# Delaying one step of a feed-forward eviction loop, and moving a quantization pass from VectorE to GpSimd

## The reference, cut

```python
def bitlinear158(x, w, b):
    xq = act_quant(rms_norm(x))      # round(x * 127/max|x|) / scale, per row
    wq = weight_quant(w)             # -1, 0, 1 times mean|w|
    return einsum('bsd,od->bso', xq, wq) + b

xn = layernorm(x)                                   # 4 x 4096 x 2048
h = silu(bitlinear158(xn, w1, b1))                  # 8192 inner columns
h = gelu(h, approximate=False)
h = layer_norm(h, ln_g, ln_b)
ffn = bitlinear158(h, w2, b2)                       # back to 2048
out = x + attention(xn) + ffn
```

## Time and profile before

| | before |
|---|---|
| median of 2 runs | 11771.39 us (11726.16 to 11816.61) |
| profiled execution | 11743.26 us |
| its span on the slowest core, core 4 | 11741.7 us |
| spans of the eight cores | 11662.1 to 11741.7 us |
| mean granted clock, core 4 | 0.765 |
| busy share PE / DVE / ACT / POOL | 45% / 31% / 19% / 2% |

### The profile page before, as it was taken

How to read it: one execution, slowest core, us unless ns; L and a number is a source line. 1 busy time by engine, 2 the same in 40 slices (tenths; PEclk the granted TensorE clock), 3 DMA queues, 4 the chain that set the end, 5 groups by cost and what they waited for, 6 DMA issues and landing times.

```text
span 11741.7 us, 91769 instructions; the slowest of 8 cores (11662.1 to 11741.7 us)
## 1 busy us (share of the span) xinstructions
PE 5257.5 (45%) x28008; PEld 3029.0 (26%) x28008; DVE 3670.1 (31%) x8144; ACT 2251.6 (19%) x4838; POOL 230.3 (2%) x214
## 2 busy tenths in 40 slices
PE   0000023454497434515455463545545465555656
PEld 0000022111133112303334242433334244222222
DVE  5421132111200122272626354362626343112020
ACT  0164442000011112212031211212031220111110
POOL 0000000111000000000000000000000000000000
PEclk9999966767688666757778686767778687777879
DMA  7789925777513554202323242322323234432324
GB/s 258 258 261 188 176 87 88 93 92 93 86 46 57 82 91 84 93 18 108 126 97 140 90 146 77 117 106 108 120 100 143 83 138 152 117 104 82 112 68 140
DMA packets 898720, 1356.88 MB, mean 116 GB/s; under 512 B 561984, under 2 KB 750784, under 8 KB 806080
## 3 DMA queue, kind: packets, MB, share of 16 engines
q1 hardware_dynamic: 495520, 1233.56, 33.3%
q0 software_dynamic: 402720, 117.45, 10.0%
HBM read 1325.70 MB, written 142.61 MB: 125 GB/s over the span
## 4 chain that ended last, share of the span: by engine, by line
DMA 35%; PE 28%; DVE 20%; ACT 7%; issue 6%; DVEq 4%; SPq 1%; ACTq 0%; POOLq 0%
PE PB L1053 9%; DMA fST<-w1q_scr 8%; DMA qW<-w2t 5%; PE PB L628 5%; PE PB L746 4%; DMA kWC<-wk 3%; DMA qW<-w1t 3%; PE PB L1461 2%; DMA tVB<-v_scr 2%; DMA fW<-w2q_scr 2%; PE PB L848 2%; DVE fTF L1354 2%; DMA q3WC<-wq 2%; DMA kt_scr<-kKO 2%; DMA y<-tOB 2%
## 5 line engine op out<-in xcount | busy, mean ns | idle before, releaser
L1053 PE MATMUL PB<-fXQT,fST 128*128 128x256 bf16 x8192 | 1289.9, 326 | 897.8 <-DMA fST<-w1q_scr 897.8
L1053 PEld LDWEIGHTS PB<-fXQT,fST 128*128 128x128 bf16 x8192 | 905.8, 115 | 1265.5 <-issue 1041.6
L848 PE MATMUL PB<-fQ,fW 128*128 128x256 bf16 x8192 | 993.7, 284 | 238.2 <-DMA fW<-w2q_scr 226.6
L848 PEld LDWEIGHTS PB<-fQ,fW 128*128 128x128 bf16 x8192 | 819.8, 102 | 414.7 <-issue 291.9
L628 PE MATMUL PB<-xnT,kWC 128*128 128x512 bf16 x2048 | 584.4, 455 | 646.0 <-ACT kKH L641 357.4
L1072 DVE TENSOR_TENSOR fTF<-PB,bcd 128x256 f32<-128x256 f32 x512 | 217.4, 425 | 1562.8 <-PE PB L1053 1560.5
L543 PE MATMUL PB<-ident_f,aXN 128*128 128x128 f32 x512 | 114.6, 416 | 1239.9 <-DVE aXN L530 991.8
L746 PE MATMUL PB<-vWV,xnT 128*128 128x512 bf16 x2048 | 483.6, 404 | 110.1 <-DMA vWV<-wv 110.1
L1090 ACT ACTIVATE fTG<-fTF 128x256 f32<-128x256 f32 x512 | 213.2, 416 | 1438.1 <-DVE fTF L1075 1437.3
L628 PEld LDWEIGHTS PB<-xnT,kWC 128*128 128x128 bf16 x2048 | 226.2, 113 | 1004.1 <-issue 855.2
L543 PEld LDWEIGHTS PB<-ident_f,aXN 128*128 128x128 f32 x512 | 103.9, 224 | 1250.3 <-issue 1250.3
(11 more groups left out here) (230 smaller groups left out, 6583.2 us busy)
## 6 DMA issues: line engine op xcount, KB each, us to landing
fST<-w1q_scr SPq DMA_DIRECT2D x128, 2048.0 KB, 7.8
fW<-w2q_scr SPq DMA_DIRECT2D x256, 1024.0 KB, 5.1
qW<-w1t SPq DMA_DIRECT2D x128, 1024.0 KB, 5.9
qW<-w2t SPq DMA_DIRECT2D x128, 1024.0 KB, 6.1
tVB<-v_scr SPq DMA_DIRECT2D x160, 512.0 KB, 3.4
kWC<-wk POOLq DMA_DIRECT2D x128, 512.0 KB, 8.0
tKB<-kt_scr SPq DMA_DIRECT2D x40, 1024.0 KB, 7.9
w1q_scr<-qT SPq DMA_DIRECT2D x64, 512.0 KB, 3.4
```

Source lines behind the costliest of these rows:

```text
L848: ins = tensor.matmul(bank[:, 0:FB], b["W2"][it % 2][:, oo * 128:(oo + 1) * 128], Q2[:, oc * FB:(oc + 1) * FB], start=(oc == 0), stop=(oc ...
L1053: ins = tensor.matmul(bank[:, 0:FB], b["ST"][0][:, dc * 512 + o4 * 128: dc * 512 + o4 * 128 + 128], XQT[:, dc * FB:(dc + 1) * FB], start=( ...
```

## The change

In the first layer, `TF` gets a second buffer (`TFP` is the pair), and DVE issues the (tanh + 1) * TF step of `oc - 1` behind the multiply and the add of `oc`, in place of the step of `oc` behind its own add. The last one follows the loop. The orders of ACT and PE stay as they are.

The 64-chunk quantization moves from DVE to POOL, with `RN` as its scratch; its waits are `f3`, the end of the previous block's second-layer matmuls, and a new count `F_hp` of normalized chunks. DVE waits at the head of the next block's first-layer loop until the quantization of the block before is done (`cq2`).

```diff
--- before.py
+++ after.py
@@ -802,7 +802,7 @@
         cw2 = ["F_w0", "F_w1"]
         cm2, cm2e, cffn = "F_m2", "F_m2e", "F_ff"
         cbt, cbe = "F_bt", "F_be"
-        REL = [csx, csd, cq1, "F_Ttp", "F_Tte", ctt, cst0, cm1, cm1e, ctg, cgl,
+        REL = [csx, csd, cq1, "F_Ttp", "F_Tte", ctt, cst0, cm1, cm1e, ctg, cgl, "F_hp",
                chz, chh, chb, chs, cstm, cse, ctk2, cq2, cw2[0], cw2[1], cm2,
                cm2e, cffn, cbt, cbe, "F_bs0", "F_bs1"]
         for nm in REL + [cte2, cstt, ctok, crr, cpk, crr2, cpk2, ctr2, cte3,
@@ -1067,27 +1067,36 @@
             @block.vector
             def _(vector):
                 vector.wait_ge(s.sem(fin0), s.val(fin0))
+                if fb > 0:
+                    vector.wait_ge(s.sem(cq2), fB[cq2])
+                def stt_h(oc):
+                    vector.wait_ge(s.sem(ctg), fB[ctg] + oc + 1)
+                    ins = vector.scalar_tensor_tensor(H[:, oc * FB:(oc + 1) * FB],
+                                                      b["TG"][oc % 2][:, :], 1.0,
+                                                      b["TFP"][oc % 2][:, :],
+                                                      ALU.add, ALU.mult)
+                    s.inc(ins, chh, 1)
                 for oc in range(OC):
+                    tf = b["TFP"][oc % 2]
                     vector.wait_ge(s.sem(cm1), fB[cm1] + oc + 1)
-                    ins = vector.tensor_mul(b["TF"][:, :], s.PB[oc % 2][:, 0:FB], s.bcd[:, :])
+                    ins = vector.tensor_mul(tf[:, :], s.PB[oc % 2][:, 0:FB], s.bcd[:, :])
                     s.inc(ins, cm1e, 1)
                     vector.drain()
-                    ins = vector.tensor_scalar(b["TF"][:, :], b["TF"][:, :],
+                    ins = vector.tensor_scalar(tf[:, :], tf[:, :],
                                                s.b1r_sb[:, oc:oc + 1], None, ALU.add)
                     s.inc(ins, chz, 1)
-                    vector.wait_ge(s.sem(ctg), fB[ctg] + oc + 1)
-                    vector.drain()
-                    ins = vector.scalar_tensor_tensor(H[:, oc * FB:(oc + 1) * FB],
-                                                      b["TG"][oc % 2][:, :],
-                                                      1.0, b["TF"][:, :], ALU.add, ALU.mult)
-                    s.inc(ins, chh, 1)
-                    vector.drain()
+                    vector.drain()
+                    if oc >= 1:
+                        stt_h(oc - 1)
+                        vector.drain()
+                stt_h(OC - 1)
+                vector.drain()
 
             @block.scalar
             def _(scalar):
                 for oc in range(OC):
                     scalar.wait_ge(s.sem(chz), fB[chz] + oc + 1)
-                    ins = scalar.activation(b["TG"][oc % 2][:, :], b["TF"][:, :],
+                    ins = scalar.activation(b["TG"][oc % 2][:, :], b["TFP"][oc % 2][:, :],
                                             AF.Tanh, scale=0.5)
                     s.inc(ins, ctg, 1)
                     scalar.wait_ge(s.sem(chh), fB[chh] + oc + 1)
@@ -1262,9 +1271,10 @@
                     vector.drain()
                     vector.tensor_mul(b["TF"][:, :], b["TF"][:, :], s.bcb[:, :])
                     vector.drain()
-                    vector.tensor_scalar(H[:, oc * FB:(oc + 1) * FB], b["TF"][:, :],
-                                         s.gr_sb[:, oc:oc + 1], s.brr_sb[:, oc:oc + 1],
-                                         ALU.mult, ALU.add)
+                    ins = vector.tensor_scalar(H[:, oc * FB:(oc + 1) * FB], b["TF"][:, :],
+                                               s.gr_sb[:, oc:oc + 1], s.brr_sb[:, oc:oc + 1],
+                                               ALU.mult, ALU.add)
+                    s.inc(ins, "F_hp", 1)
                     vector.drain()
                     if oc == 0:
                         vector.tensor_copy(b["RM"][:, :], H[:, 0:FB])
@@ -1345,18 +1355,19 @@
             f4 = self.bcast_row(s.srow[0:1, FB:2 * FB], s.bce[:, :], FB, 7, "F_bd",
                                 f3, s.val(f3))
 
-            @block.vector
-            def _(vector):
-                vector.wait_ge(s.sem(f3), s.val(f3))
+            @block.gpsimd
+            def _(gpsimd):
+                gpsimd.wait_ge(s.sem(f3), s.val(f3))
                 if pb >= 0:
-                    vector.wait_ge(s.sem(cm2), fB[cm2] + 2 * DC)
+                    gpsimd.wait_ge(s.sem(cm2), fB[cm2] + 2 * DC)
                 for oc in range(OC):
-                    vector.tensor_mul(b["TF"][:, :], H[:, oc * FB:(oc + 1) * FB], s.bcc[:, :])
-                    vector.drain()
-                    ins = vector.tensor_scalar(Q2[:, oc * FB:(oc + 1) * FB], b["TF"][:, :],
+                    gpsimd.wait_ge(s.sem("F_hp"), fB["F_hp"] + oc + 1)
+                    gpsimd.tensor_mul(b["RN"][:, :], H[:, oc * FB:(oc + 1) * FB], s.bcc[:, :])
+                    gpsimd.drain()
+                    ins = gpsimd.tensor_scalar(Q2[:, oc * FB:(oc + 1) * FB], b["RN"][:, :],
                                                MAGIC, MAGIC, ALU.add, ALU.subtract)
                     s.inc(ins, cq2, 1)
-                    vector.drain()
+                    gpsimd.drain()
 
             if pb >= 0:
                 emit_b_base(pb, fB)
@@ -1913,7 +1924,7 @@
                                    ("fHB0", [128, FB], BF16), ("fHB1", [128, FB], BF16),
                                    ("fHS0", [128, FB], BF16), ("fHS1", [128, FB], BF16),
                                    ("fTG0", [128, FB], F32), ("fTG1", [128, FB], F32),
-                                   ("fTF", [128, FB], F32),
+                                   ("fTF", [128, FB], F32), ("fTFP1", [128, FB], F32),
                                    ("fTF20", [128, FB], F32), ("fTF21", [128, FB], F32),
                                    ("fRM", [128, FB], F32),
                                    ("fRN", [128, FB], F32),
@@ -1927,7 +1938,8 @@
                                  ST=[a["fST0"], a["fST0"]],
                                  HB=[a["fHB0"], a["fHB1"]], HS=[a["fHS0"], a["fHS1"]],
                                  TG=[a["fTG0"], a["fTG1"]],
-                                 TF=a["fTF"], TF2=[a["fTF20"], a["fTF21"]],
+                                 TF=a["fTF"], TFP=[a["fTF"], a["fTFP1"]],
+                                 TF2=[a["fTF20"], a["fTF21"]],
                                  XNF0=a["fXN0"], XNF1=a["fXN1"],
                                  RM=a["fRM"], RN=a["fRN"],
                                  W2=[a["fW20"], a["fW21"]], FT=a["fFT"],
```

## The result

The changed kernel takes 13259.56 us in the median of 11 runs (13201.12 to 13380.15), against 11753.54 us for 10 runs of the kernel before taken with them. The ratio is 1.129, with a 95% interval of 1.124 to 1.133. Its profiled execution spans 13218.4 us on core 3, 1476.7 more than before. The forecast was slower, 12,740 us with a range of 12,350 to 13,080. The way was right, and the time lies above the range.

What follows compares the result with a forecast made beforehand. Waits, not a busy engine, were taken to set the time. First layer +1,267 us, last steps +12 and quantization -288 gave +991 on 11743.26 us: 12,734, stated as 12,740, range 12,350 to 13,080.

Steps and rivals of the forecast that it cites:

- The chain: First layer: from a step's multiply through DVE, ACT and the sums to PE's next matmuls, all bare, 3.03 us.
- the step at 5.06 and at 6.71: First layer, inside a group: bare chain plus matmuls, 5.06 us at 2.4 GHz or 6.71 us at 1.2 GHz.
- The fourth step: First layer, end of each group: the weight load follows it, so the 11.8 us between groups stay.
- The last step's 12 us: Behind step 63, the last tanh stands behind ACT's earlier work: about 1.5 us a block, 12 us.
- What the "What would show it" part named for line 1032: First layer: PE's wait for ACT's square rises from 223.9 to over 900 us, in 384 or more waits.
- The pass on POOL: Quantization of 64 chunks: 1.5 us a chunk, 96 us a pass, a gain of 288 us in all.
- The sign of being wrong: Quantization: the second part of the forecast is wrong if POOL's chunk is outside 0.9 to 2.5 us.
- the prediction's own 85.2 us: Block boundary: time from `bcc` ready to the next block's first multiply once DVE no longer quantizes, 142.5 us before.
- I take one step of three fast and two slow: First layer: clock mix giving 18.5 us for three steps, 9.9 more a group, 1,267 us in all.
- the rival with all steps slow: First layer: PE at 1.2 GHz in all bare steps, 1,475 us more, total 12,942 us; chance 12%.
- The rival of a dear POOL pass: Quantization: 160 us a pass on POOL loses 220 us, total 13,242 us; chance 6% for over 142 us.
- The rival on the other side: First layer: the longer dependency stays under the weight load, `stat_mm` waits go, quantization is hidden: 11,231 us; chance 4%.

Runs made afterwards that it cites:

- filler run: Changed kernel plus 16 matmuls with unread results in PE's idle time, in three steps of four: 12651.34 us, ratio 1.078 to the kernel before.
- the full move: Kernel before with the whole quantization on POOL and the first layer's order unchanged: 11839.01 us, ratio 1.006.
- the shared one: Kernel before with the sums issued one step later and the quantization split between POOL and DVE: 11295.72 us, ratio 0.957.

## Why the prediction was half right

The direction, the place and the mechanism of the first layer hold as they were put down. The chain was worked out at 3.03 us and stands at 3.09 at the full clock (filler run) and 3.30 at half (5663.60 to 5666.90); the step at 5.06 and at 6.71, measured 5.12 and, where all of it is at half clock, 7.00. That step was short mostly because the two sum matmuls were taken at the full clock: from 5666.38 to 5666.90 they need 0.52 us, not 0.31. With the sums at the full clock and the 16 matmuls at half it is 6.78, the median. The fourth step, 11.8 us with the weight load, is 11.63. The last step's 12 us are 11.4. The 57 us ahead of the base evictions went, and the base and the layer norm did start that much sooner. What the "What would show it" part named for line 1032 (over 900 us) is there with 1451.7; the load wait that it put near 900 is 564.0, as told above.

Two terms of the sum were mis-sized, and they carry the miss of 486 us (13,220 against 12,734 for the profiled executions): 400 and 124, of which the other stretches give back 38.

- **The pass on POOL: 288 us of gain put down, 112 us of loss measured, 400 us off.** The failing step is the price of a chunk, "I take twice it ... 1.5 us a chunk, 96 us a pass". It is 2.17 us, with a pass of 138 to 142. For the multiply the method gave 0.74 us (0.32 * 2 + 0.10) and the trace has 0.72. For the rounding it gave 0.48 (0.19 * 2 + 0.10) and the trace has 1.07. I had scaled DVE's rows by one factor, and DVE's order doesn't carry over: there the rounding is the shorter of the two, 0.29 against 0.42, and on POOL the longer. The gaps are 0.39 us a chunk (0.16 and 0.23) where I had 0.28. The bounds of 57 and 160 us did hold it. The sign of being wrong, a chunk outside 0.9 to 2.5 us, did not show, and it was set too wide to show: by the prediction's own 85.2 us DVE waits for POOL from 1.33 us a chunk on, and the gain is gone at 2.2. With 139 us in the prediction's own working the terms are 32 us lost behind block 0, 18 gained behind the six others and 42 lost in the tail: 56 us of loss. The rest of the 112 is in the rows too. 12 of them are no time lost: POOL starts its first chunk 0.3 us behind the broadcast where DVE started 1.8 behind it, so the stretches counted from that chunk begin sooner. Some 34 are the passes of blocks 0 to 6, which end 144 us behind the broadcast and not 139, for the long instructions told of above; and 9 lie in the tail behind its first matmul, for which the runs show no cause. The Trainium skill, "GPSIMD Engine Reference", section 4.1, has one-input operations about line rate. The trace disagrees: 1.07 us on POOL for what takes DVE 0.29. For the two-input operation the Trainium skill, in section 3.1 of the same page, has 1.96 times DVE's length; here, on 256 columns, it is 0.72 against 0.42, 1.7 times.
- **The first layer: 1,267 us put down, 1,391.5 measured, 124 off.** The failing step is "I take one step of three fast and two slow". Three quarters of the steps inside groups take 6.69 us or more, where 5.06 was the fast one and 6.71 the slow, and in no step behind the sums do the 16 matmuls run at the full clock throughout. This was the rival with all steps slow (1,475 us), to which I had given 12%.

The rivals' range failed by its making: each was tried with the others at their middle. The slow clock together with a dear POOL pass, two causes that have nothing to do with each other, is worth 1,475 + 12 + 56 = 1,543 us or 13,286 by the prediction's own bounds and the measured chunk, and that lay outside. The rival of a dear POOL pass came out at 13,242, nearer to the 13,220 of the profiled execution than any other, and that is luck: its first layer was 124 us too short and its POOL loss of 220 us 108 too long. The rival on the other side fell as argued: the load covers one wait in four.

## What to carry to other kernels

Where an in-order engine waits for another's result between two blocks of its own work, moving a step later anywhere in that loop has to be counted from the side of the wait: ask which earlier work the result now hangs on, and move the wait with it (one position is worth 1,547 us of the changed kernel's first layer here). Before work goes to another engine, price each form of instruction there by itself and set the pass against the time until its first reader; here the full move, which ended later than that, gained nothing, and the shared one did. Idle time on PE was paid twice in this loop, once as time and once in the clock of the work behind it (792 and 600 us).

## What the runs showed of the hardware

- Matmuls that do no useful work, put in PE's idle time, made the kernel 600 us faster: granted clock 0.61 to 0.82 in the first layer, 16 matmuls from 3.60 to 1.92 us.
- On POOL at 128x256 and float32 input, an instruction with two tensors takes 722 ns (median), one with a constant and one operation 852, one with a constant and two operations 1068; the type of the output (bf16 or float32) makes no difference. DVE has 0.42 us for the first and 0.29 for the last.
- Beside a DVE instruction with a constant on 128x2048, POOL's instructions of 722 and 1068 ns take up to 1.76 and 2.51 us: all 39 long ones of the changed kernel are there, and none is among the 971 that run beside no such instruction.
- Where DVE and POOL both multiply two tensors, POOL keeps its 722 ns and DVE's multiply goes from 0.43 to 0.78 us.
